# Self-attention scores over four PSUM banks instead of three, from the step behind the last unit of maxima

## The reference

```
att = einsum('bhtd,bhsd->bhts', q, k) * scale        # B=2, H=16, T=S=1024, D=16
att = where(causal, att, finfo.min)
y   = einsum('bhts,bhsd->bhtd', softmax(att), v)
x   = layernorm(x + y.reshape(B, T, C) @ w_proj)
x   = layernorm(x + cross_attention(x, ctx))
x   = layernorm(x + ffn(x))
```

## Time and profile before

| what | us |
|---|---|
| median of 3 runs | 905.83 (905.56 to 906.2) |
| the profiled execution | 905.99 |
| its span, first to last instruction | 904.2 |
| TensorE busy | 830.6 (92%) |
| VectorE busy | 476.8 (53%) |
| ScalarE busy | 381.3 (42%) |
| GpSimd busy | 321.3 (36%) |
| scores, L679, 384 instructions | 129.5 busy |
| exponentials, L1018, 384 instructions | 165.7 busy |
| mean granted TensorE clock | 0.943 |

### The profile page before, as it was taken

The page is one execution under the profiler, slowest core; times in us unless marked ns, Lnnn a source line. Parts: engine busy times, 40 slices in busy tenths (PEclk is TensorE's granted clock), DMA queues, the critical chain, the costliest instruction groups (busy, mean ns, idle before and its releaser), DMA issues.

```text
span 904.2 us, 14113 instructions
## 1 busy us (share of the span) xinstructions
PE 830.6 (92%) x5066; PEld 554.5 (61%) x5066; DVE 476.8 (53%) x1251; ACT 381.3 (42%) x774; POOL 321.3 (36%) x585
## 2 busy tenths in 40 slices
PE   7778988898998999999999888988989989999997
PEld 5544444334676777877777644433367667888886
DVE  4597888503776642146444778870257753117113
ACT  0566776745344411114222377766444442123210
POOL 4403325215421444435232424323343134336333
PEclk9856999959999999999999899996899999999999
DMA  9900444430000222324322034610000000000000
GB/s 300 381 1 2 176 153 141 148 120 1 1 1 2 94 94 94 116 74 160 128 107 94 25 118 163 231 52 2 1 2 1 1 2 0 1 1 24 1 1 25
DMA packets 23895, 68.70 MB, mean 76 GB/s; under 512 B 4400, under 2 KB 11568, under 8 KB 23600
## 3 DMA queue, kind: packets, MB, share of 16 engines
q1 hardware_dynamic: 23824, 67.77, 21.1%
HBM read 65.40 MB, written 13.63 MB: 87 GB/s over the span
## 4 chain that ended last, share of the span: by engine, by line
PE 76%; DVE 10%; ACT 8%; issue 3%; POOL 2%; POOLq 0%; ACTq 0%; DVEq 0%
PE bank_pair L873 26%; PE bank_pair L697 8%; PE bank_pair L679 7%; PE bank_pair L861 6%; ACT prob_s L1018 5%; PE bank_pair L791 4%; PE bank_pair L729 3%; PE bank_pair L648 3%; DVE bank_pair L1206 3%; PE bank_pair L592 3%; PE bank_pair L634 3%; DVE max_raw L1204 2%; PE bank_pair L803 2%; PE bank_pair L870 2%; PE bank_pair L780 2%
## 5 line engine op out<-in xcount | busy, mean ns | idle before, releaser
L1018 ACT ACTIVATE prob_s<-bank_pair 128x512 f32<-128x512 f32 (+3 forms) x384 | 165.7, 503 | 77.7 <-PE bank_pair L679 76.3
L1495 POOL TENSOR_TENSOR hid_lo_s<-act_raw_s,hid_hi_s 128x512 fp32r<-128x512 f32 x96 | 124.4, 1297 | 175.4 <-DVE hid_hi_s L1346 136.5
L679 PE MATMUL bank_pair<-q_t_s,k_t_s 64*128 64x512 f32 (+3 forms) x384 | 129.5, 446 | 17.3 <-ACT prob_s L1018 15.5
L1206 DVE CUSTOM_DVE_ANT_0 bank_pair<-bank_pair,causal_bf 128x128 f32<-128x128 f32 (+3 forms) x256 | 120.1, 514 | 47.6 <-PE bank_pair L648 47.1
L679 PEld LDWEIGHTS bank_pair<-q_t_s,k_t_s 64*128 64x128 f32 x384 | 62.2, 205 | 113.8 <-ACT prob_s L1018 82.0
L648 PE MATMUL bank_pair<-k_t_s,q_t_s 64*128 64x512 f32 (+3 forms) x384 | 122.1, 449 | 6.4 <-DVE max_raw L1204 3.2
L1456 POOL TENSOR_SCALAR_AFFINE_SELECT prob_s<-prob_s 128x128 f32<-128x128 f32 x256 | 72.0, 294 | 143.5 <-ACT prob_s L1018 140.8
L1346 DVE CAST hid_hi_s<-act_raw_s 128x512 fp32r<-128x512 f32 x64 | 35.9, 564 | 144.7 <-ACT act_raw_s L1085 143.8
L1085 ACT ACTIVATE act_raw_s<-bank_pair,scales 128x512 f32<-128x512 f32 x64 | 42.8, 688 | 160.2 <-PE bank_pair L873 160.2
L873 PE MATMUL bank_pair<-hid_hi_s,home_s 128*128 128x512 f32 x256 | 99.8, 390 | 0.8 <-POOL hid_lo_s L1495 0.8
L873 PE MATMUL bank_pair<-hid_lo_s,home_s 128*128 128x512 f32 x256 | 99.6, 389 | 0.0
(11 more groups left out here) (156 smaller groups left out, 1433.4 us busy)
## 6 DMA issues: line engine op xcount, KB each, us to landing
ring_s<-scratch SPq DMA_DIRECT2D x34, 512.0 KB, 3.3
home_s<-scratch SPq DMA_DIRECT2D x22, 512.0 KB, 5.9
checked_s<-in_w_ffn SPq DMA_DIRECT2D x2, 3584.0 KB, 18.2
scratch<-in_w_ffn SPq DMA_DIRECT2D x2, 2560.0 KB, 10.8
ring_moved_s<-scratch SPq DMA_DIRECT2D x10, 512.0 KB, 3.3
checked_s<-in_w_ffn SPq DMA_DIRECT2D x1, 4096.0 KB, 31.1
x_t_s<-in_x_t SPq DMA_DIRECT2D x2, 1024.0 KB, 5.4
x_tok_s<-in_x SPq DMA_DIRECT2D x2, 1024.0 KB, 9.4
```

Source lines behind the costliest of these rows:

```text
L679: mm(score_bank(s, j)[:, 0:CHUNK - q0], qkt(q, p, 1)[r, P * kb:P * (kb + 1)], qkt(q, p, 0)[r, CHUNK * c + q0:CHUNK * (c + 1)], start=True, ...
L1018: act.activation(prob[q][4 * (s % 2) + j][:, 0:n], score_bank(s, j)[:, 0:n], ACT.Exp, scale=SCALE).then_inc(S["exp_done"], 1)
L1206: dve.tensor_tensor_reduce(out=out[:, 0:left], in0=out[:, 0:left], in1=L["causal_bf"][:, CHUNK - left:CHUNK], scale=1.0, scalar=NEG, op0=A ...
L1495: pt(dst[1][:, m], act_raw[q][r % 3][:], dst[0][:, m].bitcast(F32), ALU.subtract).then_inc(S["f_lo"], 1)
```

## The change

Scores from number `LATE_SCORE` = 132 on (step 33, j = 0) use banks 2, 3, 4 and 5 in turn. Number 132 goes to bank 2, which was the bank of the last unit of maxima, and waits for all 192 reductions of the sequence instead of for an exponential. Every later score n waits for the exponential of n-4. That covers steps 33 to 47 of each of the two sequences, 120 of the 384 scores. No instruction of computing or moving is added or removed.

```
+LATE_S_BANKS = (2, 3, 4, 5)
...
+LATE_SCORE = 4 * (1 + max(max_step(p, u) for p in range(NP) for u in range(NU)))
+assert LATE_SCORE % len(S_BANKS) == 0
...
     def score_bank(s, j):
-        return S_BANK[(4 * s + j) % len(S_BANKS)]
+        n = 4 * s + j
+        if n >= LATE_SCORE:
+            return bank[LATE_S_BANKS[(n - LATE_SCORE) % 4]]
+        return S_BANK[n % len(S_BANKS)]
...
-            if 4 * s + j >= len(S_BANKS):
-                wait(pe, q, "exp_done", 4 * s + j - len(S_BANKS) + 1)
+            n = 4 * s + j
+            if n == LATE_SCORE:
+                wait(pe, q, "max_red", NU * NP)
+            if n > LATE_SCORE:
+                wait(pe, q, "exp_done", n - len(LATE_S_BANKS) + 1)
+            elif n >= len(S_BANKS):
+                wait(pe, q, "exp_done", n - len(S_BANKS) + 1)
```

## The result

| | us |
|---|---|
| before, measured beside it | 906.02 median (905.56 to 906.7) |
| changed kernel | 880.33 median of 4 (873.5 to 885.86) |
| ratio | 0.9712, 95% interval 0.9629 to 0.9795 |
| its profiled execution | 873.50, span 871.8, mean granted clock 0.972 |

The forecast was 878.0 (871 to 890). Three more sets of the same kernel gave 878.62, 878.67 and 875.86, ratios 0.9708, 0.9682 and 0.9684.

A forecast was written before the change was run, and what follows sets the result against it. TensorE's own order, with one wait a step for score 0's exponential, was taken to bound steps 33 to 47. Gains of 10.3 + 3.6 (clock) = 13.9 us a sequence, 27.8 for both, gave 878.0 us, range 871 to 890.

The forecast's parts named there:

- steps 38 to 43: Late stage S: denser steps at half clock gain 6.1 us a sequence; the clock's earlier return adds 3.6.
- The fourth score beside the third: Steps 33 to 47: head 3 runs beside head 2 without a wait, 1.0 us less a 512-column step at full clock.
- rival 4: Late steps: head 3 doesn't run beside head 2, only the waits go; 894.8 us, chance 0.06.
- What is late next at step 36: Step 36 waits for four row transfers, landing taken as 177.0; it starts at 177.2, gain 0.5 (0 to 1.2).
- Steps 36 and 37 paced by ScalarE: Exponentials and the bank 6 copy set the pace; step 38 starts at 183.3 instead of 184.84, gain until there 1.5 us.
- The clock: Late stage S: still falls at 180, but returns at about 183.5 instead of 203.95; gain 3.6 us a sequence.
- rival 3: Late stage S: clock never falls because steps 34 and 35 are denser; 876 us, chance 0.07.
- rival 2: Step 37: transposes don't rouse the clock, low for two or three steps more; 882 us, chance 0.06.
- the two terms: Steps 33 to 47, per sequence: 10.3 us at an unchanged clock, plus 3.6 from the clock's earlier return.
- The tail: Steps 46 and 47: gains 0.7 and 0.1 us; TensorE then waits about 1 us more for GpSimd's masks.
- rivals 5, 6 and 1: 5: clock stays low past the dip, 919, chance 0.02; 6: no gain, 905, 0.02; 1: clock as before, 885.4, 0.23.
- rival 1: Late stage S: clock stays as it was, 885.4 us; halfway or in one sequence only, 880 to 884; chance 0.23 together.

The follow-up runs named there:

- nopair: Changed kernel plus an idle 128-column product before each late step's fourth score, into the same bank, so head 3 can't run beside head 2: 890.71 us, 0.9834.
- order: Changed kernel with the late banks taken as 3, 4, 5, 2, so score 135 instead of 132 waits for the reductions: 877.94 us, 0.9689.
- tail: Kernel of order with the first query block's splitting for cross-attention moved behind step 47's exponentials and masks: 874.47 us, 0.9658.
- rep: The changed kernel again, unaltered, for its spread and a second trace: 878.62 us, 0.9708.
- rep2: The changed kernel again, unaltered, in the second set, for a third trace: 878.67 us, 0.9682.
- rep3: The changed kernel again, unaltered, as reference in the third set: 875.86 us, 0.9684.
- filler3: Kernel before (three banks, old waits) plus two idle 128-column identity products ahead of the fourth score of each step from 34 on: 894.53 us, 0.9874.
- wait_back: Changed kernel with four banks, but each late score waits again for the exponential of n-3: 906.25 us, 1.0013.
- hold: Kernel of order plus 17 idle identity products a sequence in steps 35, 36, 37 and 41, to hold the clock at full: 883.62 us, 0.9754.
- from42: Kernel before with four banks only from step 42 on, earlier steps left as they were: 893.38 us, 0.9829.

## Why the prediction was right, step by step

| step, one sequence | forecast gain | measured |
|---|---|---|
| steps 33 to 35, score 132's wait | 0.5, wait 0 | 0.54; wait 0.42, hidden |
| steps 36 and 37 | 1.0 | 1.0 with the dip, 2.4 without |
| steps 38 to 43 | 6.1 + 3.6 | 9.4 and 9.2 |
| steps 44 and 45 | 1.9 | 1.9 |
| step 46 to stage X | 0.8 | 0.8 |
| sum | 13.9 (15.1 if the clock never falls) | 13.8 with the dip, 15.0 without |

- *The fourth score beside the third*: shown. 0.73 us for four, 0.50 for four of 256 columns. The estimate of 1.0 less a step at full clock is met (7.95 - 6.04 for two steps). The part of it that was not a wait, 0.4 us, is shown by nopair, and rival 4, that only waits go (894.8), is out.
- *What is late next at step 36*: forecast the row transfers, landing 4.4 us behind the turn of the rows; step 36 started 4.7 behind it (175.79 - 171.10), behind 0.27 of standing still that the profile names "issue". That the transfers are that wait shows in when they are issued:

```profile
171.91 2.66 SPq L519 DMA_DIRECT2D q_t_s<-max_rows  x4
```

From the first issue to the start of step 36 are 3.88 us (175.79 - 171.91). In order, where the rows are turned and moved later, the first issue is at 172.47 and step 36 starts at 176.35, again 3.88. In all six profiles of the changed kernel, order and tail it is 3.86 to 3.88 in either sequence, while the gap in front of step 36 varies from 0.12 to 0.27. That the forecast put the landing three quarters of the way between two bounds was a guess without a working, and a lucky one: 173.24 + 3.88 = 177.1, against 177.0.
- *Steps 36 and 37 paced by ScalarE*: shown. ScalarE has no gap from 176.35 until step 38, and the chain to step 38 is the one of the forecast: exponentials of step 36, the copy of bank 6 until 178.90, TensorE's turn at 178.96 and its values until step 38 at 180.54. The forecast of the start of step 38, 1.5 us earlier relative to step 33, is what sequence 1 shows (0.54 + 1.03).
- *The clock*: the forecast kept the fall and let it come back in step 37. That is sequence 1 of the profile and both sequences of rep and rep2, one dip of 3.4 us (598.3 to 601.7; forecast 180 to 183.5). In sequence 0 of the changed kernel's profile, and of rep3's, order's and tail's too, it never fell: rival 3 holds there for one sequence of the two, and for both in none of these profiles. 1.3 us lie between them; the 1.2 of the forecast stood there without a working. For the likeliest case of the forecast, a dip in both sequences, the profiles of rep and rep2 are the measure: 27.4 and 27.3 us against 27.8.
- *Transposes and the clock* (rival 2): the low stretch of 598.3 to 601.6 begins with four transposes, 1.11 of 3.30 us, and full clock follows. Four transposes of the same line take 0.66 us at a granted clock of 1.0 in sequence 0 (178.96). The Trainium skill, TensorE: Matmul & The Clock Gate (Part 4: PE-mode transpose), says that full clock does not engage for transposes and that they don't count as busy for the gate in the same way. The first half does not hold in this trace (0.66 against 1.11 us). On the second the trace shows only that a stretch of which a third was transposes was followed by full clock; the forecast said more than its rows show when it wrote that the trace does not agree, since the other two thirds were products without a gap, and no run took the transposes away.
- *The waits that come with the round over PSUM banks*: filler3 fills them with work and takes the low stretch of 23.9 us away, wait_back puts them back and has it again. The Trainium skill, the same page (A second HAM failure mode: psum-queue depth-cycling), says that such small idles make the clock go up and down. The trace agrees that they take the clock down; here it did not go up and down but stayed low for 23.9 us.
- *Sizes of the two terms*: they depend on which is taken first, and the forecast took the overlap first. Taken the other way, the clock with the gaps filled is worth 6.2 to 6.4 (filler3), and the four banks on top of it 8.9 in sequence 0 and 7.4 in sequence 1, which has the dip (49.1 and 48.8 less 40.2 and 41.5). The sum is the same. It is no contradiction to the 3.6: steps that are shorter have less time to be slow in.
- *The tail*: 0.8 as forecast, and the wait for GpSimd's masks grew from 0.24 to 1.32, as forecast ("about 1 us more").
- *Slower, nothing, clock as before* (rivals 5, 6 and 1): out for the profiled executions.
- *Slips of the forecast*: step 40 is 512 columns wide, so of steps 38 to 40 only 38 and 39 are narrow; and 1.22 + 1.93 is 3.15, not 3.17. Nothing in the sum hangs on either.

What stays open: two of the first four executions took 884.56 and 885.86 at a mean clock of 0.957, and rep has one at 884.3 with 0.958. From the mean clock, they spent about 27 us more at 1.2 GHz than the profiled one: twice 0.043 of 883 is 76, twice 0.028 of 872 is 49. No execution of that kind is in a profile, so I can't say if it is the stretch of before in one sequence (rival 1, halfway), or another place. That such executions raised the median of the first set to 880.33, 2.3 above the forecast, can be read from its four times.

## What to carry to other kernels

Where a step issues one more product than there are PSUM banks in the round, the last waits for the first of its own step, and the visible wait is only part of the price: count the overlap that is lost (0.4 us of 1.0 here) and a clock that falls (6.9 us a sequence in the steps where it was low). A bank whose other use had ended was the better cure here; filling the gap with idle products brought back the clock alone (11 of the 27 us). One profile is one execution: the first here gave 3.6 us outside the changed steps that repeats of the same kernel did not all give. When a stretch becomes shorter, look at once for what lost its cover at its end: here a small operation queued ahead of the masks, worth 1.3 us a sequence.

## What was not expected of the hardware

- How little kept the clock low: one wait of 0.3 us a step at 1.2 GHz, TensorE busy 18.8 of 20.5 us. With it gone, 23.9 us of half clock become 3.4 or none. Which of the two happens in sequence 0 differs from execution to execution of one kernel; sequence 1 had the dip in all six profiles of the changed kernel, order and tail.
- The spread of the time follows the clock: 873.5 at 0.972, 876.09 at 0.967, 881.08 at 0.963, 885.86 at 0.957. The kernel before stayed within 904 to 907.2 in all executions but one of 900.5, whose mean clock was 0.956.
- A clock that is held at full is not yet a gain: hold had a mean clock of 0.971 and took 883.6, order 0.967 and took 877.9.
- New dips of 3.4 us came up in stage X, 3 to 4 us behind its start, in nopair (220.0 to 223.4), tail (212.4 to 215.8), filler3 (224.2) and from42 (222.4). In the first three the sequence's stage S had no low clock, in from42 it had 20.5 us of it. The kernels wait 1.5 us for VectorE (`xdiff_s`) near there, but so does the changed kernel, whose profile has no dip there: what brings the dip is open. TensorE is busy throughout it:

```profile
212.40:215.80 3.40, 3.40 (x15) 2.71 (x12) 2.28 (x4) 0.38 (x1) 0.42 (x2) 0.50 0.00 0
```
